# Layer 0's state products with large and small halves side by side in 256 columns, q divided before it is turned, sums held in PSUM, and a new order for layer 0

## The chip, the core and the metric

The program runs on one core of one Trainium2 chip. The metric is the device time of one execution, in microseconds (us). A core has a matmul engine (TensorE, PE in the profile, with its weight loads listed as PEld), and three engines for elementwise work: VectorE (DVE), ScalarE (ACT) and GpSimd (POOL). SyncE (SP) issues the DMAs here. Each engine takes its own instructions strictly in order and waits on semaphores for the others. Matmuls write to PSUM, which has eight banks of 512 float32 columns per partition; GpSimd does not use PSUM.

## The reference

Two attention layers follow each other, for 8 batches of 512 tokens and width 512. Layer 0 is the linear kind: q gets a softmax within each head, k a softmax over the tokens, and the state is k transposed times v for each of 8 heads of 64.

```python
xn = _ln(x, ln_w, ln_b)
q = xn @ Wq + bq
k = xn @ Wk + bk + (1.0 - src_mask) * -1000000.0
q = jax.nn.softmax(q.reshape(b, t, h, dh), axis=-1)
k = jax.nn.softmax(k.reshape(b, t, h, dh), axis=1)
v = ((xn @ Wv + bv) * src_mask).reshape(b, t, h, dh)
att = jnp.einsum('bnhd,bnhl->bhdl', k, v)
y = jnp.einsum('bnhd,bhdl->bnhl', q, att).reshape(b, t, d)
emb_out = (jax.nn.silu(emb) @ W_emb + b_emb)[:, None, :]
scale, shift = jnp.split(emb_out, 2, axis=2)
hh = _ln(y, ln2_w, ln2_b) * (1.0 + scale) + shift
hh = jax.nn.silu(hh) @ W_out + b_out
return x + hh
```

Layer 1 has the same frame round an ordinary softmax attention with 16 heads of 32.

## The kernel before

Every float32 product is made from two rounded parts (`float32r`): a large part (name ending in h) and the small rest (l). A product A times B is three matmuls, Ah Bh, Ah Bl and Al Bh (`product`, L491). Each pass of `product` multiplies 128x128 weights with 512 columns.

The work of one batch in layer 0 is cut into named steps, and one list sets the order for all engines: `the_order` weaves tracks of steps by the guessed cost in `COST` and by start and end fractions. Each engine walks that list and issues its share. In a batch b of layer 0:

- `tx` turns x (16 transposes on PE), ACT writes the large part `xTh` and a full copy `tb` (L766, L769), DVE writes the rest `xTl` (L1024).
- `k` (16 passes, then on DVE mask and maximum, on ACT Exp into `ET`), `v` (16 passes; DVE adds the bias into `vt`, ACT writes `vh`, DVE writes `vl`: L1077, L802, L1080), `te` (turns `ET`; ACT writes `Eh`, DVE `El`, L785 and L1056), `q` (16 passes; DVE bias and maximum L1090 and L1094, POOL subtracts it L1284, ACT Exp into `eq` L809).
- `st` makes the state: for each of 4 column groups and 4 token tiles the three matmuls L581, L582, L583 with 128 columns. `sta` then scales it by the sums of k and splits it into `Ah` and `Al` (L1105, L817, L1110). `Ah` is 130 columns wide: two extra columns of ones make the sums of each q row on PE.
- In batch b+1's k stretch, `y` turns `eq`, splits it (`qh` on ACT L825, `ql` on DVE L1116), multiplies it with the state (L603, L604, L605, 130 columns), and DVE divides by the q sums (L1126, L1130).
- `ny` normalises y (statistics on DVE, L1277 on POOL), `ty` turns it and makes silu, with DVE writing into `yb` twice (L1140, L1143), ACT `sTh` (L842), DVE `sTl` (L1148). `o` (16 passes) multiplies with W_out; DVE adds x and SP stores.

PSUM banks are handed out in the same list (`the_banks`): eight banks rotate in the order in which they come free, and `done` names the semaphore that frees one. Layer 1 has its own table of fractions and is bounded by a chain of matmuls, maxima (L1170), exponentials (L885) and sums (L1325); it shares `tx`, `v`, `ty` and `o` with layer 0.

The state part of PE's program is

```python
for t in range(NT):
    e.matmul(bank[:, n], Eh[:, t, n], vh[:, t, n], start=(t == 0), stop=False)
    e.matmul(bank[:, n], Eh[:, t, n], vl[:, t, n], start=False, stop=False)
    r = e.matmul(bank[:, n], El[:, t, n], vh[:, t, n], start=False, stop=(t == NT - 1))
```

Of the kernel before, what the change touches and what calls it, by code (L numbers as in the profile page):

```python
# [5 lines left out]
ALU = mybir.AluOpType  # L6
ACT = mybir.ActivationFunctionType
# [22 lines left out]
    "k": MM + (0.0,), "v": MM + (0.1, 0.2, 0.0), "q": MM + (0.3, 0.0), "o": MM + (0.0,),  # L30
# [5 lines left out]
    "stacks": (0.0,), "ahead": (0.0,), "narrow": (0.0,), "end": (0.0,),  # L36
# [4 lines left out]
PLAN = {  # L41
    "att": ((0.03, 0.83), (0.03, 0.83), (0.1, 0.97), (0.03, 0.83)),
# [35 lines left out]
def the_order():  # L78
# [19 lines left out]
    for b in range(B):  # L98
        past, first, last = b >= 1, b == 0, b + 1 == B
        yb = [("y", b - 1, g) for g in range(5)] if past else []  # L100
        if last:
            o.append((("ahead",), 0))
        weave(o, (tiles("k", b), 0, 1), (yb, 0.05, 1), ([] if first else [("nx", b + 1)], 0.3, 0.9),
              (wpart(0, "v") if first else [], 0.2, 0.9), (first_m[0] if first else [], 0.9, 1.0))
        weave(o, (tiles("v", b), 0, 1), (tiles("te", b), 0.18, 0.85), ([("ny", b - 1)] if past else [], 0, 0.8),
# [66 lines left out]

def bank_uses(p, i):
# [50 lines left out]
def temp_uses(order):  # L224

    last, before = {}, {}
    for p, i in order:
        if i == 0 and (p[0] == "tx" or (p[0] == "ty" and p[2] < NC)):
            before[p] = last.get(p[2] % 2)
            last[p[2] % 2] = p  # L230
    return before


# [15 lines left out]
def cond_two_layers(nc, A, out):  # L249
# [4 lines left out]
    temp_before = temp_uses(order)  # L254
    with ctx:
# [61 lines left out]
        vh = sb("vh", [128, NT, D], FR, c=c0)  # L317
        vl = sb("vl", [128, NT, D], FR, c=c0)
# [5 lines left out]
        Ah = sb("Ah", [128, NC, 130], FR, c=c0)  # L324
        Al = sb("Al", [128, NC, 130], FR, c=c0)
# [8 lines left out]
        yrc = sb("yrc", [128, 2, 4], c=c0)  # L334
# [3 lines left out]
        for i in range(2):  # L338
# [17 lines left out]
            "att", "a_set", "A_sc", "A_hi", "A_lo", "q_tr", "qT_hi", "qT_lo", "y_mm", "y_rc", "y_sc",  # L356
# [17 lines left out]
        def temp_free(p):  # L374

            k = temp_before[p]
            if k is None:
                return None
            return s["xT_lo" if k[0] == "tx" else "y_s"], 4 * k[1] + k[2] + 1

        def done(key):
# [4 lines left out]
            if k == "v":  # L386
                return s["v_add"], 4 * key[1] + key[2] + 1
# [92 lines left out]
        def _(e):  # L480
# [1084 lines left out]
```

## Time and profile before

| | us |
|---|---|
| median of 3 runs | 1534.92 |
| their range | 1533.7 to 1539.51 |
| the profiled execution | 1538.86 |
| its span | 1536.9 |

| engine | busy us | share of the span |
|---|---|---|
| PE | 1430.6 | 93% |
| PEld | 1011.7 | 66% |
| DVE | 1018.9 | 66% |
| ACT | 776.9 | 51% |
| POOL | 757.4 | 49% |

The span is the time from the first to the last instruction; the profiled execution took 2 us more than its span. Matmuls overlap in the records: each lasts longer than the distance to the next one, so for PE the distance between starts is what to read, not the duration. A row of the timeline gives start, duration, engine, line and operation, and in brackets the idle time before it with what ended it. A row of the windows view gives a stretch and, for each engine, busy time and number of instructions in it, then the granted clock of PE as a share of full speed. Layer 0 runs from about 15 to 515 us, 61 us per batch, and layer 1 from there to the end.

### The profile page before, as it was taken

How to read it: one execution, taken by the hardware profiler on the slowest of the kernel's cores; microseconds unless marked ns; L12 is line 12 of the kernel's file. 1: busy time of each engine (PE TensorE's matmuls, PEld its weight loads, DVE VectorE, ACT ScalarE, POOL GpSimd, SP SyncE). 2: the span in 40 equal slices, each digit the busy share in tenths (PEclk: the TensorE clock that was granted, in tenths of full speed). 3: DMA queues.
4: the chain of work that ended last, by engine and by line, in shares of the span. 5: the costliest groups of instructions: out<-in, count | busy, mean ns of one | idle time of the engine just before them, and what ended most of it. 6: DMA issues, size and time to landing. Idle time of an engine off the chain costs nothing.

```text
span 1536.9 us, 21020 instructions
## 1 busy us (share of the span) xinstructions
PE 1430.6 (93%) x7296; PEld 1011.7 (66%) x7296; DVE 1018.9 (66%) x1929; ACT 776.9 (51%) x1305; POOL 757.4 (49%) x660
## 2 busy tenths in 40 slices
PE   6999999999999798998998998998998999999985
PEld 4788888888888675565565565565565665565543
DVE  5687777778778675647657557556656656746654
ACT  5334334334344435555646646645755655564561
POOL 0222333233222325557656765774675765846852
PEclk9899999999999899998999999999999999999996
DMA  8011121111222266553354335335434434533320
GB/s 311 5 58 55 35 90 55 35 55 35 90 76 69 70 172 178 164 138 103 96 125 130 103 106 149 92 104 144 109 90 140 122 97 124 131 103 97 106 73 28
DMA packets 83914, 156.19 MB, mean 102 GB/s; under 512 B 8264, under 2 KB 8264, under 8 KB 83808
## 3 DMA queue, kind: packets, MB, share of 16 engines
q1 hardware_dynamic: 83808, 154.84, 35.2%
q8 instruction: 58, 0.95, 0.3%
q14 instruction: 48, 0.39, 0.1%
HBM read 104.45 MB, written 50.36 MB: 101 GB/s over the span
## 4 chain that ended last, share of the span: by engine, by line
PE 66%; DVE 18%; issue 6%; POOL 5%; ACT 5%; DMA 0%; POOLq 0%; ACTq 0%; SPq 0%; DVEq 0%
PE ps L494 13%; PE ps L496 12%; PE ps L495 11%; PE ps L651 6%; PE ps L685 6%; PE ps L668 6%; DVE cT L1170 6%; PE ps L489 4%; DVE st L1011 3%; POOL yb L1277 2%; DVE yb L1143 1%; PE ps L706 1%; DVE yb L1140 1%; ACT Pb L885 1%; PE ps L605 1%
## 5 line engine op out<-in xcount | busy, mean ns | idle before, releaser
L1325 POOL TENSOR_TENSOR Pb<-Pb 128x512 f32<-128x512 f32 x376 | 471.0, 1293 | 182.9 <-PE ps L685 109.3
L1170 DVE TENSOR_REDUCE cT<-ps 128x1 f32<-128x512 f32 x512 | 325.5, 683 | 93.5 <-PE ps L651 93.3
L885 ACT ACTIVATE Pb<-ps 128x512 f32<-128x512 f32 x512 | 282.3, 611 | 204.6 <-PE ps L668 186.8
L651 PE MATMUL ps<-Ks,Qs 98*128 98x512 f32 x512 | 198.8, 433 | 16.3 <-DVE sg_q L1162 12.0
L668 PE MATMUL ps<-Qs,Ks 106*128 106x512 f32 x512 | 186.9, 417 | 5.6 <-ACT Qs L868 1.6
L651 PEld LDWEIGHTS ps<-Ks,Qs 98*128 98x128 f32 x512 | 97.0, 195 | 107.9 <-DVE cT L1170 40.9
L1256 POOL TENSOR_TENSOR rs<-ve,mhalf 128x4 f32<-128x4 f32 x32 | 33.0, 1032 | 248.3 <-DVE ve L997 152.8
L668 PEld LDWEIGHTS ps<-Qs,Ks 106*128 106x128 f32 x512 | 96.6, 190 | 63.6 <-ACT Pb L885 21.7
L1284 POOL TENSOR_TENSOR vt<-vt,qmx 128x512 f32<-128x512 f32 x32 | 33.4, 1045 | 163.1 <-DVE qmx L1094 163.1
L494 PE MATMUL ps<-Wh_o,sTh 128*128 128x512 f32 x256 | 109.8, 429 | 4.1 <-DVE sTl L1148 3.6
L494 PE MATMUL ps<-xTh,Wh_k 128*128 128x512 f32 x256 | 109.9, 429 | 1.6 <-DVE Wl_k L950 1.4
L494 PE MATMUL ps<-Wh_v,xTh 128*128 128x512 f32 x256 | 105.7, 413 | 0.0
L496 PE MATMUL ps<-Wh_o,sTl 128*128 128x512 f32 x256 | 104.3, 407 | 0.0
L495 PE MATMUL ps<-Wl_o,sTh 128*128 128x512 f32 x256 | 103.7, 405 | 0.0
L496 PE MATMUL ps<-xTh,Wl_k 128*128 128x512 f32 x256 | 103.1, 403 | 0.0
L495 PE MATMUL ps<-xTl,Wh_k 128*128 128x512 f32 x256 | 102.8, 401 | 0.0
L496 PE MATMUL ps<-Wh_v,xTl 128*128 128x512 f32 x256 | 100.8, 394 | 0.0
L495 PE MATMUL ps<-Wl_v,xTh 128*128 128x512 f32 x256 | 100.2, 391 | 0.0
L1291 POOL TENSOR_TENSOR wr<-wr,boB 128x512 f32<-128x512 f32 x64 | 93.4, 1478 | 12.7 <-DMA wr<-in_x 12.6
L1024 DVE TENSOR_TENSOR xTl<-tb,xTh 128x512 fp32r<-128x512 f32 x64 | 54.4, 850 | 60.9 <-ACT tb L769 60.9
L1156 DVE TENSOR_TENSOR wr<-ps,wr 128x512 f32<-128x512 f32 x64 | 43.9, 686 | 71.5 <-PE ps L496 71.3
L1162 DVE SCALAR_TENSOR_TENSOR sg_q<-ps,cols,sg_q 128x512 fp32r<-128x512 f32 x32 | 23.7, 742 | 89.3 <-ACT sg_q L860 89.3
(176 smaller groups left out, 3102.2 us busy)
## 6 DMA issues: line engine op xcount, KB each, us to landing
Qs<-stack_scratch SPq DMA_DIRECT2D x96, 256.0 KB
Ks<-stack_scratch SPq DMA_DIRECT2D x96, 256.0 KB
stack_scratch<-sg_q SPq DMA_DIRECT2D x32, 512.0 KB, 2.8
stack_scratch<-sg_k SPq DMA_DIRECT2D x32, 512.0 KB, 3.1
wr<-in_x SPq DMA_DIRECT2D x32, 256.0 KB, 5.3
x_scratch<-wr SPq DMA_DIRECT2D x32, 256.0 KB, 2.0
wr<-x_scratch SPq DMA_DIRECT2D x32, 256.0 KB, 3.7
out<-wr SPq DMA_DIRECT2D x32, 256.0 KB, 2.0
```

What stands on the lines that cost most here:

```text
L489: r = e.transpose(bank[:, t * 128:(t + 1) * 128], src, ident)
L494: e.matmul(bank[:], lh(k), rh(k), start=(k == 0), stop=False)
L495: e.matmul(bank[:], lh(k), rl(k), start=False, stop=False)
L496: return e.matmul(bank[:], ll(k), rh(k), start=False, stop=(k == NC - 1))
L651: e.matmul(bank[:], Qs[par][0:RX, j, t * 128:(t + 1) * 128], Ks[par][0:RX, j, :], start=True, stop=True).then_inc(s["S"], 1)
L668: e.matmul(bank[:], Ks[par][0:RE, j, m * 128:(m + 1) * 128], Qs[par][0:RE, j, :], start=True, stop=True).then_inc(s["ST"], 1)
L685: r = e.matmul(PV[32 * j:32 * j + 32, :], xbuf(8 + b)[:, m, h * 32:(h + 1) * 32], pb[:, j, :], start=(m == 0), stop=(m == NT - 1))
L885: e.activation(p_buf(n, m)[:, j, :], ps[bank_of["a", n, m, j]][:], ACT.Exp).then_inc(s["P"], 1)
L1024: e.tensor_tensor(xTl[:, c, :], tb[c % 2][:], xTh[:, c, :].bitcast(F32), ALU.subtract).then_inc(s["xT_lo"], 1)
L1170: e.tensor_reduce(nx[:, n % 2, j, t, 0:1], ps[bank_of["S", n, j, t]][:], AX.X, ALU.max, negate=True).then_inc(s["S_max"], 1)
L1291: e.tensor_tensor(wr[t][:], wr[t][:], boB[:], ALU.add).then_inc(s["xb"], 1)
L1325: e.tensor_tensor(acc[:, j, :], acc[:, j, :], p_buf(n, m)[:, j, :], ALU.add).then_inc(s["Ps_pool"], 1)
```

## The change

1. State and y products. `vh`/`vl` become one tile `vhl`, `Ah`/`Al` one tile `Ahl`, with the large and small part of the same 128 columns next to each other. The two matmuls with the same weights become one with 256 columns; its two halves land in separate columns of PSUM and are added afterwards. Two matmuls (256 and 128 columns) replace three. The state takes two banks instead of one.
2. The additions: ACT copies the small half out (`A_c1`, `y_c1`), DVE adds it to the large half (`A_sc`, `y_sc`).
3. The columns of ones are gone. q is divided by its sum before it is turned: a new step `qn` per token tile sums (DVE) and inverts (DVE), and POOL multiplies `eq`. The division by the k sums moves from the state into the copy of the turned q (`qh`, `ql`).
4. Intermediates stay in PSUM: the full copy of x (`xT_f`), v with its bias, and u in `ty` are written back into the bank they were read from, which stays taken for longer. `tb` and `vt` are no longer used there. This holds for layer 1 too.
5. The fractions for layer 0's tracks move into `PLAN` with new values, and GpSimd's memset of ones (`ones`) moves from `stacks` to behind the last `y`.

```diff
 PLAN = {
+    "0k": ((0.134, 0.71), (0.313, 1.065)),
+    "0v": ((0.56, 1.051), (0, 0.565)),
+    "0q": ((0.109, 0.992), (0, 0.247), (0.978, 0.998)),
...
-            return s[("k_exp", "v_lo", "q_exp")[r // 4]], 4 * c + r % 4 + 1
+            return s[("k_exp", "q_exp")[r // 4]], 4 * c + r % 4 + 1
...
             if k == "v":
-                return s["v_add"], 4 * key[1] + key[2] + 1
+                return s["v_lo" if key[1] < 8 else "v_hi"], 4 * key[1] + key[2] + 1
...
             if k == "ty":
-                return s["y_u"], 4 * key[1] + key[2] + 1
+                return s["s_lo" if in_bank(key[1]) else "y_s"], 4 * key[1] + key[2] + 1
...
                 for t in range(NT):
-                    e.matmul(bank[:, n], Eh[:, t, n], vh[:, t, n], start=(t == 0), stop=False)
-                    e.matmul(bank[:, n], Eh[:, t, n], vl[:, t, n], start=False, stop=False)
-                    r = e.matmul(bank[:, n], El[:, t, n], vh[:, t, n], start=False, stop=(t == NT - 1))
+                    e.matmul(out, Eh[:, t, n], vhl[:, t, :, n], start=(t == 0), stop=False)
+                    r = e.matmul(out[:, 0:128], El[:, t, n], vhl[:, t, 0, n], start=False, stop=(t == NT - 1))
...
-                        n, o_ = slice(t * 128, (t + 1) * 128), bank[:, u * 130:(u + 1) * 130]
-                        e.matmul(o_, a[:, n], Ah[:, g, :], start=True, stop=False)
-                        e.matmul(o_, a[:, n], Al[:, g, :], start=False, stop=False)
-                        r = e.matmul(o_, l[:, n], Ah[:, g, :], start=False, stop=True)
+                        n, o_ = slice(t * 128, (t + 1) * 128), bank[:, u * 256:(u + 1) * 256]
+                        e.matmul(o_, a[:, n], Ahl[:, g, :, :].rearrange("p s n -> p (s n)"), start=True, stop=False)
+                        r = e.matmul(o_[:, 0:128], l[:, n], Ahl[:, g, 0, :], start=False, stop=True)
...
-                    e.activation(tb[c % 2][:], bank[:], ACT.Identity, scale=p[:, c:c + 1], bias=p[:, 4 + c:5 + c]).then_inc(s["xT_f"], 1)
+                    e.wait_ge(s["xT_hi"], 4 * x + c + 1)
+                    e.activation(bank[:], bank[:], ACT.Identity, scale=p[:, c:c + 1], bias=p[:, 4 + c:5 + c]).then_inc(s["xT_f"], 1)
...
                         part = ps[bank_of["st", b, u]][r, :].rearrange("p (g s n) -> p g s n", g=2, s=2)
+                        e.copy(Af[r, 2 * u:2 * u + 2, :], part[:, :, 1, 64 * h:64 * h + 64]).then_inc(s["A_c1"], 1)
...
-                    e.copy(qh[g % 2][:], ps[bank_of["tq", b, g]][:]).then_inc(s["qT_hi"], 1)
+                    e.activation(qh[g % 2][:], ps[bank_of["tq", b, g]][:], ACT.Identity,
+                                 scale=krc[:, b % 2, g:g + 1]).then_inc(s["qT_hi"], 1)
...
+                    e.copy(yb[:, 2 * half:2 * half + 2, g * 128:(g + 1) * 128], y3[:, :, 1, :]).then_inc(s["y_c1"], 1)
...
-                    e.tensor_tensor(vt[t % 2 if x < 8 else 0][:], ps[bank_of["v", x, t]][:], bvB[:], ALU.add).then_inc(s["v_add"], 1)
+                    e.tensor_tensor(ps[bank_of["v", x, t]][:], ps[bank_of["v", x, t]][:], bvB[:], ALU.add).then_inc(s["v_add"], 1)
...
+            def qn(i, b, t):
+                n = 4 * b + t + 1
+                e.wait_ge(s["q_exp"], n)
+                e.tensor_reduce(qdn[:, t % 2, :], eq[:, t, :].rearrange("p (h d) -> p h d", h=H0), AX.X, ALU.add).then_inc(s["q_den"], 1)
...
+                e.reciprocal(qrc[:, t % 2, :], qdn[:, t % 2, :]).then_inc(s["q_rc"], 1)
...
+                    yv = yb[:, 2 * half:2 * half + 2, g * 128:(g + 1) * 128]
+                    e.tensor_tensor(yv, y3[:, :, 0, :], yv, ALU.add).then_inc(s["y_sc"], 1)
...
-                        e.tensor_scalar(yv, t4(ps[bank_of["ty", x, c]]), mod[:, 0, c, bb:bb + 1], mod[:, 1, c, bb:bb + 1],
+                        u = ps[bank_of["ty", x, c]]
+                        e.tensor_scalar(u[:], u[:], mod[:, 0, c, bb:bb + 1], mod[:, 1, c, bb:bb + 1],
```

How the new order stands on PE, at the border from v to q in batch 2 of layer 0 (psN are banks, `Wh_q,xTh` and its like are the passes of q, `identr,yb` turns y of the batch before, `vh,Eh` is the first state matmul). Before:

```order
L489 MATMUL ps3<-identr,yb 128x128 x4
L494 MATMUL ps6<-Wh_q,xTh 128x512
L495 MATMUL ps6<-Wl_q,xTh 128x512
L496 MATMUL ps6<-Wh_q,xTl 128x512
L494 MATMUL ps0<-Wh_q,xTh 128x512
L495 MATMUL ps0<-Wl_q,xTh 128x512
L496 MATMUL ps0<-Wh_q,xTl 128x512
L489 MATMUL ps7<-identr,yb 128x128 x4
L494 MATMUL ps0<-Wh_q,xTh 128x512
L495 MATMUL ps0<-Wl_q,xTh 128x512
L496 MATMUL ps0<-Wh_q,xTl 128x512
L581 MATMUL ps5<-vh,Eh 128x128
```

And now, from the last turn of the k exponentials (`identr,ET`):

```order
L486 MATMUL ps5<-identr,ET 128x128 x4
L491 MATMUL ps4<-Wh_q,xTh 128x512
L492 MATMUL ps4<-Wl_q,xTh 128x512
L493 MATMUL ps4<-Wh_q,xTl 128x512
L486 MATMUL ps0<-identr,yb 128x128 x4
L486 MATMUL ps3<-identr,yb 128x128 x4
L491 MATMUL ps4<-Wh_q,xTh 128x512
L492 MATMUL ps4<-Wl_q,xTh 128x512
L493 MATMUL ps4<-Wh_q,xTl 128x512
```

Behind the last row stand one more turn of y and then the first state matmul. Before, six passes of q and three turns of y stood between the last v product and the first state matmul; now the last turn of `ET`, two passes and three turns of y.

On PE at the start of batch 2's k stretch, where y of the batch before begins. Before, the second turn of `eq` with what follows it; the first turn stands three passes of k ahead of it:

```order
L489 MATMUL ps2<-identr,eq 128x128 x4
L494 MATMUL ps7<-xTh,Wh_k 128x512
L495 MATMUL ps7<-xTl,Wh_k 128x512
L496 MATMUL ps7<-xTh,Wl_k 128x512
L494 MATMUL ps7<-xTh,Wh_k 128x512
L495 MATMUL ps7<-xTl,Wh_k 128x512
L496 MATMUL ps7<-xTh,Wl_k 128x512
L603 MATMUL ps0<-Ah,qh0 128x130
```

Now, from the first turn:

```order
L486 MATMUL ps5<-identr,eq 128x128 x4
L491 MATMUL ps4<-xTh,Wh_k 128x512
L492 MATMUL ps4<-xTl,Wh_k 128x512
L493 MATMUL ps4<-xTh,Wl_k 128x512
L486 MATMUL ps1<-identr,eq 128x128 x4
L491 MATMUL ps0<-xTh,Wh_k 128x512
L492 MATMUL ps0<-xTl,Wh_k 128x512
L493 MATMUL ps0<-xTh,Wl_k 128x512
L600 MATMUL ps2<-Ahl,qh0 128x256
L601 MATMUL ps2<-Ahl,ql0 128x128
```

Between the first turn and the first y matmul there are two passes and one turn now, and five passes and one turn before.

On DVE at the border from q to o in batch 1. Before:

```order
L1090 TENSOR_TENSOR vt<-ps,bqB 128x512
L1094 TENSOR_REDUCE qmx<-vt 128x8
L1105 TENSOR_TENSOR Af<-ps,krc 64x256 x2
L1110 TENSOR_TENSOR Al<-Af,Ah 64x4x64 x2
L1024 TENSOR_TENSOR xTl<-tb,xTh 128x512
L1156 TENSOR_TENSOR wr<-ps,wr 128x512
```

And now, with the sums of q (`qdn`) and their inverses around the state's additions and splits:

```order
L1097 TENSOR_TENSOR vt<-ps,bqB 128x512
L1101 TENSOR_REDUCE qmx<-vt 128x8
L1107 TENSOR_REDUCE qdn<-eq 128x8
L1111 RECIPROCAL qrc<-qdn 128x8
L1107 TENSOR_REDUCE qdn<-eq 128x8
L1111 RECIPROCAL qrc<-qdn 128x8
L1119 TENSOR_TENSOR ps<-ps,Af 64x2x64 x4
L1126 TENSOR_TENSOR Ahl<-ps,Ahl 64x2x64 x4
L1107 TENSOR_REDUCE qdn<-eq 128x8
L1111 RECIPROCAL qrc<-qdn 128x8
L1036 TENSOR_TENSOR xTl<-ps,xTh 128x512
```

The four instructions of two `qn` steps stand ahead of the state's, so the state and the next batch's x come later in DVE's queue by their length.

## Rows read from the trace of the kernel before

**Rows 1.** Windows: stretch, busy us (count) of PE, PEld, DVE, ACT, POOL, clock

```profile
50.00:111.00 61.00, 57.28 (x299) 50.15 (x298) 43.63 (x114) 22.13 (x39) 17.99 (x22) 0.86 0.12 40
111.00:172.00 61.00, 60.88 (x346) 51.71 (x345) 48.51 (x102) 23.03 (x41) 20.17 (x20) 1.00 0.19 57
```

**Rows 2.** Waits of PE, 50 to 480 us: us in total, times, longest

```profile
PE ps L489 <- POOL xin L1268: 3.6, 1, 3.6
```

**Rows 3.** Timeline of PE, 281 to 284 us: start, duration

```profile
280.82 0.22 PE L603 MATMUL ps<-Ah,qh 128*128 128x130 f32 x1
280.88 0.27 PE L604 MATMUL ps<-Al,qh 128*128 128x130 f32 x1
280.99 0.27 PE L605 MATMUL ps<-Ah,ql 128*128 128x130 f32 x1
...
282.18 0.22 PE L603 MATMUL ps<-Ah,qh 128*128 128x130 f32 x1
...
283.31 0.39 PE L496 MATMUL ps<-Wh_v,xTl 128*128 128x512 f32 x1
283.54 0.39 PE L494 MATMUL ps<-Wh_v,xTh 128*128 128x512 f32 x1
```

**Rows 4.** Timeline of PE, 40 to 42 us: matmuls of 8 columns

```profile
40.55 1.03 PE L517 MATMUL ps<-pick,sp 128*128 128x8 f32 x8
41.43 0.48 PE L494 MATMUL ps<-Wh_v,xTh 128*128 128x512 f32 x1
```

**Rows 5.** Windows of batch 0's state and the stretches behind it

```profile
60.00:66.00 6.00, 2.66 (x13) 2.69 (x14) 1.77 (x3) 2.02 (x4) 5.20 (x6) 0.65 0.00 0
66.00:70.00 4.00, 4.00 (x21) 4.00 (x21) 1.42 (x3) 3.41 (x6) 0.00 (x0) 0.50 0.00 0
```

**Rows 6.** Timeline of PE, 64 to 65 us

```profile
64.33 0.41 PE L582 MATMUL ps<-vl,Eh 128*128 128x128 f32 x1
64.55 0.41 PE L583 MATMUL ps<-vh,El 128*128 128x128 f32 x1
```

**Rows 7.** Timeline of PE, end of v and first state matmul

```profile
295.46 0.39 PE L496 MATMUL ps<-Wh_v,xTl 128*128 128x512 f32 x1
...
301.50 0.22 PE L581 MATMUL ps<-vh,Eh 128*128 128x128 f32 x1
```

**Rows 8.** Timeline of ACT and DVE, the last v tile of that batch

```profile
296.70 0.72 ACT L802 ACTIVATE vh<-vt,mk 128x512 fp32r<-128x512 f32 x1 [1.77 <-DVE vt L1077]
```

**Rows 9.** The same on DVE

```profile
297.46 0.75 DVE L1080 SCALAR_TENSOR_TENSOR vl<-vt,mk,vh 128x512 fp32r<-128x512 f32 x1 [0.79 <-ACT vh L802]
```

**Rows 10.** Groups of DVE, 111 to 480 us: count, busy us, mean ns, idle before

```profile
L1024 DVE TENSOR_TENSOR xTl<-tb,xTh 128x512 fp32r<-128x512 f32 x24 | 25.4, 1058 | 9.8 <-ACT tb L769 9.8
L1094 DVE TENSOR_REDUCE qmx<-vt 128x8 f32<-128x512 f32 x24 | 16.5, 686 | 2.5
L1056 DVE TENSOR_TENSOR El<-ps,Eh 128x512 fp32r<-128x512 f32 x22 | 14.8, 675 | 0.0
L1126 DVE RECIPROCAL yrc<-ps 128x4 f32<-128x4 f32 x48 | 8.4, 174 | 10.5 <-PE ps L605 10.1 <-issue 0.2
L1031 DVE TENSOR_SCALAR mB<-mB 128x512 f32<-128x512 f32 x5 | 3.6, 730 | 0.0
```

**Rows 11.** Groups of POOL, 111 to 480 us

```profile
L1284 POOL TENSOR_TENSOR vt<-vt,qmx 128x512 f32<-128x512 f32 x24 | 25.1, 1045 | 98.8 <-DVE qmx L1094 98.8
```

**Rows 12.** Waits of PE from 600 to 1500 us, layer 1

```profile
PE ps L659 <- DVE nxs L1188: 21.0, 9, 2.7
```

**Rows 13.** Timeline of DVE in layer 1, 711 to 718 us

```profile
711.11 0.69 DVE L1143 SCALAR_TENSOR_TENSOR yb<-tb,yb 128x512 f32<-128x512 f32 x1
...
715.01 1.10 DVE L1143 SCALAR_TENSOR_TENSOR yb<-tb,yb 128x512 f32<-128x512 f32 x1
...
717.25 0.19 DVE L1188 TENSOR_REDUCE nxs<-cT 128x16 fp32r<-128x32 f32 x1
```

**Rows 14.** Groups of DVE, 590 to 1500 us

```profile
L1024 DVE TENSOR_TENSOR xTl<-tb,xTh 128x512 fp32r<-128x512 f32 x28 | 19.4, 692 | 34.3 <-ACT tb L769 34.3
```

More of the change, by code:

```diff
@@ L35 @@
     "tl": (0.2, 0.1, 0.9, 1.1), "tlx": (1.0, 0.0, 0.4, 0.4, 0.4, 0.4),
-    "stacks": (0.0,), "ahead": (0.0,), "narrow": (0.0,), "end": (0.0,),
+    "stacks": (0.0,), "ones": (0.0,), "ahead": (0.0,), "narrow": (0.0,), "end": (0.0,),
 }
 PLAN = {
+    "0k": ((0.134, 0.71), (0.313, 1.065)),
+    "0v": ((0.56, 1.051), (0, 0.565)),
+    "0q": ((0.109, 0.992), (0, 0.247), (0.978, 0.998)),
+    "0o": ((0.012, 0.839), (0.012, 0.907), (0.012, 0.288)),
     "att": ((0.03, 0.83), (0.03, 0.83), (0.1, 0.97), (0.03, 0.83)),
@@ L108, in the_order @@
         state = tiles("st", b) + [("sta", b)]
-        weave(o, (tiles("q", b), 0, 1), ([] if first else state, 0.35, 1),
-              ([("ty", b - 1, c) for c in range(5)] if past else [], 0, 0.75),
+        weave(o, (tiles("q", b), 0, 1), ([] if first else state, *PLAN["0q"][0]), ([("qn", b, 0), ("qn", b, 1)], *PLAN["0q"][2]),
+              ([("ty", b - 1, c) for c in range(5)] if past else [], *PLAN["0q"][1]),
               ([("mb", 0, 1)] if first else [], 0, 0.5), ([("nx", 1)] if first else [], 0.1, 0.7),
@@ L113, in the_order @@
         if not last:
-            weave(o, (tiles("o", b - 1) if past else state, 0.05, 1), (tiles("tx", b + 1), 0, 0.9),
-                  (wpart(0, "o") if first else [], 0.3, 1))
+            weave(o, (tiles("o", b - 1) if past else state, *PLAN["0o"][0]), (tiles("tx", b + 1), *PLAN["0o"][1]),
+                  (wpart(0, "o") if first else [], 0.3, 1), ([("qn", b, 2), ("qn", b, 3)], *PLAN["0o"][2]))
     o.append((("stacks",), 0))
     weave(o, (tiles("o", B - 2), 0, 0.5), (tiles("tx", 8), 0, 0.35), (wpart(1, "q"), 0, 0.5),
+          ([("qn", B - 1, 2), ("qn", B - 1, 3)], 0.02, 0.35),
           ([("y", B - 1, g) for g in range(5)], 0.45, 1), ([("qk", 0, 0), ("qk", 0, 1)], 0.65, 0.95))
+    o.append((("ones",), 0))
     o.append((("stack", 0), 0))
@@ L221, in the_banks @@
     return bank, before
[L224 to L231, printed above, removed]
 def raw_items():
@@ L831, in ty @@
                         e.wait_ge(s["e_mod"], 16 * (x // 8 + 1))
-                    if (f := temp_free(("ty", x, c))) is not None:
-                        e.wait_ge(*f)
+                    if n >= 2:
+                        e.wait_ge(s["y_s"], n - 1)
                     e.wait_ge(s["yn_tr"], n + 1)
@@ L1038, in k @@
                         if b >= 2:
-                            e.wait_ge(s["A_sc"], 2 * (b - 1))
-                    if (f := kvq_before(b, g)) is not None:
+                            e.wait_ge(s["A_sc"], 4 * (b - 1))
+                    if (f := kq_before(b, g)) is not None:
                         e.wait_ge(*f)
```

170 lines of the change are left out of this document (87 added, 83 removed).

## The prediction, made before the changed kernel was run

> **What bounds the kernel now.** I read the busy times by stretch first. In a steady batch of layer 0, 61 us, PE is busy for 60.88 us and DVE for 48.51 [rows 1]; then the waits of PE: over seven batches the only one of size is a single 3.6 us for x of batch 1 [rows 2]. So layer 0 is bounded by how fast PE issues, and the distances between starts are the prices. In [rows 3] a whole 512-column matmul takes 283.54 - 283.31 = 0.23 us. Between the L603 at 280.82 and that at 282.18 lie six small matmuls (130 columns) and one pass of k, three wide ones: 1.36 - 0.69 = 0.67 us, 0.111 each. The reader is to see that this is not the price of 130 columns: eight matmuls of 8 columns take 41.43 - 40.55 = 0.88 us, 0.11 each as well [rows 4]. So up to some width a matmul with new 128x128 weights costs 0.11 us whatever its columns.
>
> Two places leave the pattern. Batch 0's state runs at half clock: PE idles 3.6 us [rows 2], the granted clock averages 0.65 over 60 to 66 us and is 0.50 (1.2 of 2.4 GHz) over 66 to 70 although PE is busy throughout [rows 5], and small matmuls then start 64.55 - 64.33 = 0.21 us apart (0.213 over a run of them) [rows 6]. And layer 1 is bounded by a chain over several engines, not by PE.
>
> **The pairs in place of triples.** State: 16 triples in each of 8 batches; y: 16 in each of 8. A triple costs 3 x 0.111 = 0.333 us. A pair costs 0.111 for the 128-column matmul and W for the 256-column one, which no row shows. Below, W is 0.11 (the weights' price); above, the straight line through 128 columns at 0.111 and 512 at 0.231 gives 0.151. I take 0.116, half the price of 512 columns, since the floor in [rows 4] shows that the line's constant part is not added. A pair is 0.227, and each saves 0.106.
> - 7 batches of state and 7 of y at full clock: 224 x 0.106 = 23.7 us.
> - Batch 0's state: 16 triples at half clock are 10.2 us. The new order puts the first state group ahead of the turn that waits for x, so 4 pairs run inside the old idle time, and 12 pairs of 2 x 0.213 cost 5.1. Gain 5.1.
> - Batch 7's y lies where layer 1 begins, with other waits. I count its 16 pairs at the full-clock price, 1.7.
>
> The Trainium skill ("TensorE: Matmul & The Clock Gate", "Back-to-back issue gap") gives N/2.4 + 2.5 ns for an isolated matmul: 56 ns for 128 columns, 109 for 256. By that a triple would be 167 and a pair 165 ns, and the change would gain nothing on PE. Here 128 columns take 111 ns, so the isolated gap does not bound; its section on LDWEIGHTS (128 columns of weights / 1.2 = 107 ns) does agree with the 0.11 in both groups. A pair at 107 + 109 would save 0.117 and the first line would be an estimated 26.2 in place of 23.7.
>
> **New waits of PE.** With PE at 61 - 32 x 0.106 = 57.6 us per batch, what was hidden has less cover, and the order itself tightens two places.
> - v to state. Before, the first state matmul starts 301.50 - 295.69 = 5.8 us after the last v product has been issued, at 295.46 + 0.23 [rows 7], and `vl` of the last tile ends at 298.21 [rows 9]. Now only the last turn of `ET` (4 x 0.11), two passes (1.38) and three turns (1.32) lie between: 3.1 us. The chain it must cover: that turn done at 0.72 (0.44 and the tail of its last matmul), ACT's `Eh` at the 0.72 of [rows 8]: 1.44 us; DVE's `El` 0.68, the mask 0.73 [rows 10] and `vl` 0.75 [rows 9] behind it: 3.6 us. The wait is 0.5.
> - The first y matmul. Before, five passes and a turn cover the split of the turned q; now two passes and a turn, 1.82 us. The split is an ACT instruction with a scale, 0.72, and a DVE one with a scalar, 0.75, behind a tail of 0.3: 1.77. With what DVE has in its queue I take 0.3.
> Together 0.8 us in each of 7 batches: 5.6 us. The bounds are 0 (DVE a little earlier everywhere) and 2 us a batch.
>
> **DVE, ACT, POOL.** DVE gets four sums and inverses, 4 x (0.686 + 0.17), 3.4 us a batch; it loses 8 inverses of 0.174 = 1.4, and 4 x (1.058 - 0.686) = 1.5 as `xTl` no longer reads two SBUF tiles while POOL works [rows 10]. In layer 1 the same instruction took 0.692 [rows 14]. The state's additions and splits are twice as many at half the size, about even. So 48.5 becomes 49 of 57.6 us: 85%. ACT gets eight copies of 256 columns and the state's, some 5 us on its 23 [rows 1]; POOL four multiplications of 1.045 [rows 11] on its 20. None bounds. `qn` 0 and 1 delay DVE's state work and the next x by 1.7 us at the end of q; o's 16 passes and four turns (12.8 us on PE) come behind, with 7.2 us of DVE work (four `xTl`, four additions, the other two `qn`), and cover that. The state takes two banks, and v and ty stay in theirs until the split is done; counted in PE's program at these prices, 4.8 us or more lie between the step that gives up a bank and its next use. The moved `ones` I price at nothing, as POOL is busy for a third of a batch [rows 1]. If o's cover is gone, k's first pass would be late by up to those 1.7 us.
>
> **Layer 1.** Banks are held longer by one ACT or DVE instruction and I found none whose next user comes that soon. One gain: `L1143` reads two SBUF tiles and took 0.69 to 1.10 us and more under POOL's load; the one at 715.01 stands ahead of the last maximum, and so of `nxs` at 717.25 [rows 13], for which PE waits (21.0 us in 9 waits [rows 12]). With u in PSUM it should be 0.69: 0.41 x 7 = 2.9 us. Bounds 0 and 7.
>
> **The sum.** -23.7 - 5.1 - 1.7 + 5.6 - 2.9 = -27.8. The profiled execution took 1538.86 (span 1536.9), 3.9 above the median, so this is 1511.1 there and 1534.92 - 27.8 = 1507.1 for the median. Forecast **1507**.
>
> **Rivals.**
> 1. Columns are what is paid: 256 cost 0.222. For it, 128 columns and 2 x 0.111; against, the 8-column rows. Then all three gains on PE go: 1534.9 + 5.6 - 2.9 = 1537.6, no change. 5%.
> 2. DVE's waits come to the front. It is idle 61 - 48.5 = 12.5 us a batch, in part waiting for ACT (0.79 before `vl` [rows 9]) in a fixed order. If all of that stayed, a batch would be 49 + 12.5 = 61.5 us and nothing would be left; halfway, 2 us a batch: 1534.9 - 33.4 + 14 = 1515.5. 20%.
> 3. Slower: a new wait in each batch lets the clock fall. One wait of 3.6 us cost batch 0 more than itself: the stretch with it issued 299 matmuls against 346 [rows 1], 47/346 x 61 = 8.3 us. Seven of these: 1534.9 - 33.4 + 58.1 = 1559.6. Its place would be k's first pass behind `qn` and the state's work on DVE. It decides from a loss of 4.8 us a batch (33.4 / 7). Against it: the cover of o above. 5%.
> 4. The clock stays up in batch 0, as 0.9 us of the 3.6 are now filled. The state would run at 0.227 a pair: 2.4 us less, and the turns and passes behind it about as much: 1502. 10%.
>
> **How the numbers follow.** The forecast case has 60%. What a measurement of this kernel can tell from no change is about 0.5%, 7.7 us. W at its upper end adds 224 x 0.035 = 7.8, waits of 2 us add 8.4; no waits, W at 0.11 and 7 us in layer 1 take off 5.6, 1.3 and 4.1. The range 1497 to 1522 holds cases 2 and 4 and either end alone. Faster: 60 + 20 + 10 and a little of the rest, 0.91; the same 0.05; slower 0.04.
>
> **What would show it.** L579 and L600 start 0.116 us ahead of their partners at full clock, L580 and L601 0.111; a steady batch is 58.4 us; PE's waits list the first state matmul behind `vl` with about 0.5 us and the first y matmul behind `ql`; `xTl` in layer 0 takes 0.69; PE's wait for `nxs` falls from 21 to about 18 us. I am wrong if a 256-column matmul costs 0.15 or more, if PE's waits in layer 0 exceed 2 us a batch, or if layer 1 moves by more than 7 us.

## The result, and the profile after

The changed kernel takes 1495.74 us, the median of 4 runs (1493.2 to 1501.43), where the kernel before took 1534.57 in runs beside it. The ratio is 0.9746, 95% interval 0.9708 to 0.9783: 38.8 us less, where 27.8 were forecast, and 1.3 us below the range. The profiled execution took 1493.49 us, its span is 1491.7.

Windows of one steady batch of layer 0 in the changed kernel (columns as in [rows 1]):

```profile
243.50:302.00 58.50, 58.50 (x322) 49.66 (x321) 48.43 (x106) 28.50 (x57) 21.80 (x25) 1.00 0.19 59
```

PE has no idle time left; DVE is at 83%, ACT has got 28.5 us. The same batch of the kernel before:

```profile
257.00:319.30 62.30, 62.14 (x354) 52.91 (x353) 49.14 (x102) 24.28 (x43) 20.16 (x21) 1.00 0.16 56
```

A batch was 62.3 us there, not the 61 that I used, which was only the width of the windows in [rows 1]. Pairs of the state on PE, start and duration:

```profile
281.13 0.36 PE L579 MATMUL ps<-vhl,Eh 128*128 128x256 f32 x1
281.33 0.22 PE L580 MATMUL ps<-vhl,El 128*128 128x128 f32 x1
281.39 0.33 PE L579 MATMUL ps<-vhl,Eh 128*128 128x256 f32 x1
281.56 0.22 PE L580 MATMUL ps<-vhl,El 128*128 128x128 f32 x1
281.62 0.34 PE L579 MATMUL ps<-vhl,Eh 128*128 128x256 f32 x1
```

A pair repeats after 281.62 - 281.39 = 0.23 us, where a triple took 0.333 [rows 3]. The waits of PE from 50 to 480 us (total, times, longest), answering to [rows 2]:

```profile
PE ps L486 <- POOL xin L1275: 2.7, 1, 2.7
PE ps L600 <- DVE ql L1132: 1.5, 1, 1.5
PE ps L579 <- issue: 1.4, 1, 1.4
PE ps L491 <- DVE xTl L1036: 0.6, 1, 0.6
```

None of them comes back in each batch. Batch 0's state and what follows, answering to [rows 5]:

```profile
60.00:66.00 6.00, 3.35 (x20) 3.21 (x19) 4.30 (x8) 1.66 (x3) 6.00 (x8) 0.75 0.00 0
66.00:70.00 4.00, 4.00 (x22) 4.00 (x21) 2.38 (x6) 3.93 (x7) 3.19 (x4) 0.53 0.00 0
70.00:78.00 8.00, 5.98 (x33) 4.34 (x32) 6.99 (x16) 7.01 (x17) 0.43 (x1) 1.00 0.45 132
```

The granted clock is back at 1.00 from 70 us. The stretch at 0.50 was 17 us long before (61.7 to 78.8 us) and is 7 now (63.0 to 69.8).

DVE groups, `xTl` of layer 0 and u's product of layer 1, answering to [rows 10, 13]:

```profile
L1036 DVE TENSOR_TENSOR xTl<-ps,xTh 128x512 fp32r<-128x512 f32 x24 | 16.4, 684 | 3.1 <-ACT ps L764 3.1
...
L1151 DVE SCALAR_TENSOR_TENSOR yb<-tb,ps 128x512 f32<-128x512 f32 x28 | 19.2, 687 | 1.0
```

and the second one before, from 590 to 1500 us, which I had read at only two places:

```profile
L1143 DVE SCALAR_TENSOR_TENSOR yb<-tb,yb 128x512 f32<-128x512 f32 x28 | 36.9, 1316 | 1.0
```

By the times at which `xTl` of each batch starts, the profiled executions differ by 5.8 us at batch 2, then by 3.8 more per batch, 29.5 at batch 8, 31.3 at batch 9 and 45.2 at the end. So layer 0 gave 31 us. Layer 1 gave 14 between these two executions, 7 to 8 by the medians (38.8 - 31.3). Executions of one kernel differ, and they differ with the mean granted clock: the four of the changed kernel took 1493.2, 1493.5, 1498.0 and 1501.4 us at 0.973, 0.976, 0.970 and 0.965.

### The profile page after: what moved, and what is told of

It is laid out like the page before. It is cut to its first block, busy times and chain, and to the rows that moved or that the text cites. A ratio compares the mean times of both kernels' runs of the same rounds, so it can differ in the third digit from the quotient of the medians.

```text
span 1491.7 us, 20585 instructions
## 1 busy us (share of the span) xinstructions
PE 1387.8 (93%) x7040; PEld 969.7 (65%) x7040; DVE 999.6 (67%) x1958; ACT 811.8 (54%) x1417; POOL 772.1 (52%) x692
## 4 chain that ended last, share of the span: by engine, by line
PE 66%; DVE 16%; ACT 8%; issue 5%; POOL 3%; DMA 1%; SPq 0%; POOLq 0%; ACTq 0%; DVEq 0%
PE ps L491 13%; PE ps L493 12%; PE ps L492 12%; PE ps L647 7%; PE ps L681 7%; PE ps L664 6%; DVE cT L1177 6%; PE ps L486 4%; ACT xTh L762 2%; DVE st L1023 2%; ACT ps L764 2%; PE ps L702 1%; DVE ps L1148 1%; PE ps L600 1%; ACT Pb L901 1%
## 5 line engine op out<-in xcount | busy, mean ns | idle before, releaser
L1304 POOL TENSOR_TENSOR wr<-wr,boB 128x512 f32<-128x512 f32 x64 | 82.2, 1297 | 13.6 <-DMA wr<-in_x 13.6
L1169 DVE SCALAR_TENSOR_TENSOR sg_q<-ps,cols,sg_q 128x512 fp32r<-128x512 f32 x32 | 23.8, 742 | 88.5 <-ACT sg_q L876 88.5
L1036 DVE TENSOR_TENSOR xTl<-ps,xTh 128x512 fp32r<-128x512 f32 x64 | 44.0, 688 | 51.3 <-ACT ps L764 51.1
```

Of the source, the lines that this page charges most:

```text
L1036: e.tensor_tensor(xTl[:, c, :], ps[bank_of["tx", x, c]][:], xTh[:, c, :].bitcast(F32), ALU.subtract).then_inc(s["xT_lo"], 1)
L1304: e.tensor_tensor(wr[t][:], wr[t][:], boB[:], ALU.add).then_inc(s["xb"], 1)
```

## The experiments

Each run stands beside runs of the kernel before on its own chip. Times are compared as ratios to it, and a difference in us is that of ratios times 1534.6. The changed kernel stands at 0.9746, and the interval of its own ratio is 6 us either way, so a difference against it is known to 6 to 8 us; one between two of the other kernels to 3 to 5. The medians of the kernel before, by which the ratios are taken, lay between 1534.4 and 1538.1 us, both of these on the same chip. Where a difference is smaller than that, the delays in the traces decide.

**Pairs and order, a square of four kernels.** First, pairs undone:

```diff
-                    e.matmul(out, Eh[:, t, n], vhl[:, t, :, n], start=(t == 0), stop=False)
+                    e.matmul(out[:, 0:128], Eh[:, t, n], vhl[:, t, 0, n], start=(t == 0), stop=False)
+                    e.matmul(out[:, 128:256], Eh[:, t, n], vhl[:, t, 1, n], start=False, stop=False)
```

and the same in y.

> The changed kernel with one part undone: each 256-column matmul of the state and of y is two of 128 columns again (same weights, same halves, same PSUM columns); order, q's division and all else stay. If the pairs are the gain of layer 0 (0.333 us for a triple, 0.230 for a pair in the trace), 224 pairs at full clock cost 224 x 0.103 = 23 us, batch 0's 16 cost 3 to 5 and batch 7's y 1.7: the time rises by 28 to 30 us, to about 1524, and a steady batch of layer 0 goes from 58.5 to 61.8 us. If the new order is the gain and PE's small matmuls have slack around them, it rises by less than 15 us.

Measured: 1527.12 us, ratio 0.9920 (0.9897 to 0.9942), +26.7 us. Then the order undone:

```diff
-    "0k": ((0.134, 0.71), (0.313, 1.065)), "0v": ((0.56, 1.051), (0, 0.565)),
-    "0q": ((0.109, 0.992), (0, 0.247), ..., "0o": ((0.012, 0.839), (0.012, 0.907), ...
+    "0k": ((0.05, 1), (0.3, 0.9)), "0v": ((0.18, 0.85), (0, 0.8)),
+    "0q": ((0.35, 1), (0, 0.75), ..., "0o": ((0.05, 1), (0, 0.9), ...
```

> The changed kernel with layer 0's tracks at the fractions of the kernel before (the two new q steps stay where they are). The prediction charged the new order with 5.6 us of waits, which the trace does not show. If the order was put right for the new lengths, the old one costs: the waits of PE in layer 0 grow by 0.5 to 2 us a batch and the time rises by 4 to 14 us. If the order carries nothing, the time stays within 2 us of the changed kernel. If my charge was real and hidden only in other terms, the time falls by up to 5 us.

Measured: 1527.17 us, ratio 0.9923 (0.9895 to 0.9950), +27.2 us: twice what I thought possible. Then both:

> The changed kernel with both parts undone: 128-column triples and the old fractions; what is left of the change is the division of q, the sums in PSUM and the copies on ACT. It closes the square of order and pairs: undoing the pairs alone cost 26.7 us and undoing the order alone 27.2. If the two gains are independent, this costs 54 us, 15 slower than the kernel before. If each hides the other (with triples PE is late enough for the old order's waits to be covered, and with the old order the pairs' time is waited away), it costs little more than either alone, 27 to 39 us, and a steady batch of layer 0 is again 62 us with few waits.

Measured: 1531.46 us, ratio 0.9965 (0.9951 to 0.9979), +33.6 us. So in the old order the pairs are worth 33.6 - 27.2 = 6.4 us, and with triples the new order is worth 6.9; together they are worth 33.6. The delays at batch 8 in the traces say the same: 22.6, 24.1 and 30.3 us. Each is the condition of the other. With both undone, what is left of the change still makes the kernel 5.4 us faster than the one before. One batch of the first kernel (new order, triples) and of the second (old order, pairs) in windows shows why:

```profile
254.60:316.40 61.80, 61.80 (x353) 53.04 (x352) 48.42 (x107) 28.76 (x57) 21.80 (x25) 1.00 0.18 56
```

```profile
252.60:314.40 61.80, 59.28 (x322) 49.53 (x321) 48.24 (x107) 27.96 (x57) 22.09 (x25) 1.00 0.18 56
```

The same 61.8 us, once with PE busy throughout, once with the pairs' time returned as idle time. The waits of PE in the second, 111 to 480 us:

```profile
PE ps L600 <- DVE ql L1132: 7.9, 6, 1.9
PE ps L486 <- ACT ET L772: 7.6, 6, 1.4
```

ACT's last exponential is late because its input is. DVE there (idle time and what ended it in brackets):

```profile
214.20 1.09 DVE L1140 TENSOR_TENSOR yb<-ps,yb 128x256 f32<-128x256 f32 x3 [1.14 <-ACT yb L841]
215.21 0.68 DVE L1058 CUSTOM_DVE_ANT_0 vt<-ps,mB 128x512 f32<-128x512 f32 x1
```

DVE idles 1.14 us for ACT's copy of the small half of y, a hand-over that part 2 of the change brought, with k's last maximum (L1058) queued behind it. This is the mechanism of my second rival; with the new order, all else equal, neither wait is there. Which stretch does it? Two of the four were tried alone, v and k:

> The changed kernel with the old fractions in the v stretch alone (the turns of the exponentials begin at 0.18 of it again and not at 0.56). With all the old fractions PE waited 1.27 us a batch for the last exponential (ET) before those turns. If that wait comes from the turns' place, this alone brings it back: 7 x 1.3 = 9 us or somewhat more. If it comes from what stands ahead on ACT (y's copies in the k stretch), this alone brings less than 3 us.

> The changed kernel with the old fractions in the k stretch alone (y from 0.05 to 1 of it and not from 0.134 to 0.71). With all the old fractions PE waited 1.2 us a batch at the first y matmul for the split of the turned q. If the wait comes from y's early start, this alone brings 7 x 1.2 = 8 to 10 us. And y's eight copies then end late in ACT's queue, ahead of the last exponential: if that is what made ET late, PE waits for it here too, and the cost is 14 us or more.

Measured: 0.9809 (0.9781 to 0.9837) and 0.9766 (0.9726 to 0.9806), by the medians +9.7 and +3.1 us, but up to batch 8 their traces are only 2.9 and 6.1 us late, against 24.1 with all the old fractions. PE's wait for `ET` is 0.5 us over six batches with the old v alone and absent with the old k alone. So neither of these two makes it alone. For v the trace fits the second case that I had set (less than 3 us), for k neither; the stretches of q and o were not tried alone, and which combination is the least is open.

**Batch 0.** The state behind the turn again, in batch 0 alone:

```diff
-            weave(o, (tiles("o", b - 1) if past else state, *PLAN["0o"][0]), (tiles("tx", b + 1), *PLAN["0o"][1]),
+            weave(o, (tiles("o", b - 1), *PLAN["0o"][0]) if past else (state, 0.05, 1), (tiles("tx", b + 1), *(PLAN["0o"][1] if past else (0, 0.9))),
```

> The changed kernel with batch 0's state behind the turn that waits for x of batch 1, as in the kernel before; nothing else moves. The prediction put about 2 us of its 5.1 on the four pairs that run inside the old idle time. If the shorter wait (2.7 for 3.6 us) also keeps the clock up (7 us of half clock there against 17.5), this costs 5 us or more; if only the four pairs moved, 1 to 2 us; if neither, nothing.

Measured: 1499.64 us, ratio 0.9748 (0.9728 to 0.9769): nothing, and batch 2's `xTl` starts within 0.3 us of the changed kernel's. The four pairs in the idle time gain nothing. The length of the half clock there goes with the pairs: in the seven kernels with triples (the kernel before included) that stretch is 10 to 17 us long, in the ten with pairs and no dummies at that wait 3 to 7 in all. Why it does is not shown.

**Widths.** A series behind the last o (its weights differ from one matmul to the next):

```diff
+            for width in (8, 64, 128, 192, 256, 320, 384, 448, 512):
+                for i in range(24):
+                    probe(width, i)
```

> The changed kernel with a series behind its last o: 48 matmuls of 512 columns, then 24 each of 8, 64, 128, 192, 256, 320, 384, 448 and 512 columns, each with other 128x128 weights, then 12 pairs of 256 and 128 columns. The whole is longer by the series, so only the distances between starts are read. If a matmul costs the larger of the weights' price and its columns, 8 to 256 columns are 0.11 to 0.12 us apart, 512 are 0.23, and 384 lie at 0.17. If a fixed part is added to the columns, 256 lies near 0.15. A pair should be 0.227 to 0.231.

Measured, in a single run, mean distance between starts in us: 8 columns 0.108, 256 0.120, 320 0.147, 384 0.174, 448 0.206, 512 0.229; a pair 0.227. The 64, 128 and 192 came out at 0.18 to 0.215, for the reason that the windows show (busy time and count of PE, then the granted clock), in the middle of the 8, 64 and 128 columns, at the end of the 192, and in the middle of the 256 and 384:

```profile
1500.00:1505.00 5.00, 5.00 (x28) 1.00 0.00 0
...
1507.00:1511.00 4.00, 4.00 (x24) 0.58 0.00 0
1511.50:1516.00 4.50, 4.50 (x23) 0.50 0.00 0
...
1521.20:1521.30 0.10, 0.10 (x2) 0.65 0.00 0
1521.30:1521.40 0.10, 0.10 (x3) 1.00 0.00 0
1521.50:1524.00 2.50, 2.50 (x23) 1.00 0.03 7
...
1528.00:1531.50 3.50, 3.50 (x22) 1.00 0.00 0
```

(The first row is the 512-column lead-in and the start of the 8 columns.) PE is busy for every bit of these windows, and still the clock falls, at 1507.6 us, 0.8 us into the 64 columns. It stays at half through the 128 and the 192 columns and is full again from 1521.3, when the last of the 192 columns start (at 1521.31) and before the first of the 256 (1521.42). Why it fell and rose at these places is not shown. Above 256 columns the time goes by columns: 0.229 for 512, 0.174 for 384; below lies a floor of 0.11. The Trainium skill ("TensorE: Matmul & The Clock Gate", "Back-to-back issue gap") has N/2.4 + 2.5 ns, 109 for 256 columns, as the isolated gap; with new weights each time the series shows 120. The 107 ns that follow from its section on LDWEIGHTS (128 columns / 1.2) are close to the floor.

**Layer 1: u in PSUM.** Undone in the changed kernel for batches 8 to 14, and done alone in the kernel before:

```diff
-                        e.tensor_scalar(u[:], u[:], mod[:, 0, c, bb:bb + 1], ...
...
+                        u = src[:] if in_bank(x) else yb[:, :, c * 128:(c + 1) * 128]
+                        e.tensor_scalar(u, ..., mod[:, 0, c, bb:bb + 1], ...
```

(`src` is the bank.) The bank of `ty` is given up one instruction sooner with u in SBUF, and one later with u in PSUM.

> The changed kernel with one part undone in layer 1: for batches 8 to 14 u is written into yb again, so that the instruction after it reads two SBUF tiles and the bank is given up one instruction sooner. If this read is what moved layer 1 (1.32 us on average against 0.69), it goes back to 1.3 us, PE's wait for nxs in the fifth, ninth, ... chain step grows from 2.3 to 2.7 us, the granted clock falls behind it again as in the kernel before, and the time rises by 7 to 10 us. If my term was right in size it rises by 3 us. If layer 1 gained from something else (x or v held in PSUM), it stays within 1 us.

> The kernel before with that one part of the change alone: in layer 1 u stays in the PSUM bank. If it is the whole gain of layer 1, the time falls by 7 to 10 us, to about 1526, and the low-clock stretches of 7 us behind the wait for nxs shrink or go. If my term was right in size it falls by 3 us; if something else moved layer 1, by less than 1 us.

Measured: 1503.82 us, 0.9769 (0.9745 to 0.9793), +3.5 us against the changed kernel, and 1532.91 us, 0.9967 (0.9950 to 0.9984), 5.1 us less than the kernel before. The part gives `yb<-tb,yb` back its 1327 ns and takes it to 686 in the other, so the whole change of that instruction is this part's. The first time, known to 7 us, decides nothing, and the second lies between the two stories.

What the length of that instruction depends on can be read exactly. The third and fourth of a batch on DVE in the kernel before (the first, at 711.11, and the second, at 715.01, stand in [rows 13]), and what GpSimd does then:

```profile
718.18 1.70 DVE L1143 SCALAR_TENSOR_TENSOR yb<-tb,yb 128x512 f32<-128x512 f32 x1
...
720.64 1.79 DVE L1143 SCALAR_TENSOR_TENSOR yb<-tb,yb 128x512 f32<-128x512 f32 x1
```

```profile
714.28 1.27 POOL L1291 TENSOR_TENSOR wr<-wr,boB 128x512 f32<-128x512 f32 x1
...
718.05 1.28 POOL L1291 TENSOR_TENSOR wr<-wr,boB 128x512 f32<-128x512 f32 x1
720.61 1.27 POOL L1304 TENSOR_TENSOR sTl<-yb,sTh 128x512 fp32r<-128x512 f32 x1 [1.28 <-ACT sTh L842]
```

The first of the four runs while GpSimd is idle and takes 0.69. Each of the others starts while a GpSimd instruction runs and ends about 0.55 us after it: 715.55 and 716.11, 719.33 and 719.88, 721.88 and 722.43. It is so for all 23 that start beside a GpSimd instruction in batches 8 to 15 of this trace. In the changed kernel, with u in PSUM, they take 0.69 beside the same work. So the four of a batch take 0.69, 1.07, 1.71 and 1.79 us, 2.5 more than four of 0.69, and 2.1 of these lie on the third and fourth.

**The clock in layer 1.** From batch 1 of layer 1 on, PE waits for long twice in each batch: 1.7 us for `sg_q`, the small half of q, and 2.3 (before: 2.7) for `nxs`, the reduced maxima. In the changed kernel the half clock follows 9 of these 14 waits, at least one in each batch; in the kernel before 11 of 14. Dummy matmuls ahead of both waits (here the second; 14 stand ahead of the first), written into the bank that the waiting matmul overwrites:

```diff
+                    if n % 4 == 1 and n > 4:
+                        for _ in range(18):
+                            e.matmul(bank[:, 0:128], identr[:], identr[:], start=True, stop=True)
                     e.wait_ge(s["nx_lo"], n + 1)
```

> The kernel before with dummy matmuls ahead of the two waits of PE that come back in each batch of layer 1 from the second on (14 of 128 columns before the first S matmul, 18 before the one that reads nxs, written into the bank that the waiting matmul overwrites): at 0.11 us each they last 1.5 and 2.0 us, a little less than the waits of 1.7 and 2.7 us. If the idle time itself is what makes the clock fall, the half-clock stretches behind these waits shrink or go, and the time falls by up to 7 batches x (3.5 + 7) us / 2 = 30 us, by 10 us or more. If the clock follows something else, the time does not fall, and it rises by what the dummies overrun the wait, 0 to 5 us.

> The changed kernel with the same dummy matmuls. The waits are 1.7 and 2.3 us and the low-clock stretches behind them 3.5 us and, in some batches, 3.5 us more. If idle time makes the clock fall, the time falls by 5 to 15 us, to about 1485, and this version beats both kernels. If the clock follows something else, it stays or rises by up to 5 us.

Measured: in the kernel before 1528.76 us, ratio 0.9938 (0.9926 to 0.9950), 9.5 us less. In the changed kernel **1481.03**, ratio 0.9628 (0.9616 to 0.9640), 18 us below the changed kernel by the ratios, 14.7 by the medians and 12.2 between the two traces: the fastest kernel here. Its four runs lie within 0.9 us, those of the changed kernel within 8, and from x of batch 10 to x of batch 15 each batch takes 115.9 to 116.2 us, where it took 117.0 to 118.5. 26 us of batch 9, changed kernel and changed kernel with dummies (the dummies are among the counts, and the second kernel is 3 us further on in its batch):

```profile
666.00:692.00 26.00, 21.71 (x104) 13.93 (x103) 21.64 (x43) 17.25 (x28) 20.60 (x19) 0.93 0.52 142
```

```profile
666.00:692.00 26.00, 24.83 (x135) 15.67 (x133) 21.26 (x40) 18.22 (x30) 21.63 (x19) 1.00 0.56 152
```

With the idle time filled the clock stays up behind these waits: between 600 and 1440 us the changed kernel has 31 us at half clock, the one with dummies 1. What the dummies leave of the two waits (17.0 and 12.0 us) is 0.9 and 4.3. PE's waits from 600 to 1440 us, changed kernel and with dummies:

```profile
PE ps L655 <- DVE nxs L1195: 17.0, 8, 2.3
PE ps L647 <- DVE sg_q L1169: 12.0, 7, 1.7
```

```profile
PE ps L650 <- ACT Pb L907: 4.5, 14, 0.4
PE ps L650 <- DVE sg_q L1175: 4.3, 7, 0.6
...
PE ps L661 <- DVE nxs L1201: 0.9, 1, 0.9
```

Then dummies at the other long waits, 42 of 512 columns before the last y among them:

> The changed kernel with the dummies of the earlier run, and further ones of 512 columns (0.23 us each) ahead of PE's other long waits, each a little shorter than its wait: 10 before x of batch 1 (2.7 us), 26 before the first turn of batch 7's q (6.4), 6 before batch 7's y (1.7), 15 and 5 before the second and third nxs (3.7 and 1.4), and 42 before the last y (10.6). 45 us of half clock were left there. If idle time is what lowers the clock in these places too, the time falls by 5 to 15 us below the earlier 1481; if they are bounded by other engines' chains, it stays within 2 us of it.

Measured: 1481.67 us, ratio 0.9642 (0.9621 to 0.9664), no gain. The half clock of the whole execution went from 51 to 15 us, the mean clock of the last 39 us from 0.74 to 0.90, and nothing came of it. By what I had set before the run, those places are bounded by other engines' chains; which ones was not traced.

**The sizes with the clock held.** The three undoings and the mirror once more, each with the two groups of dummies, against 0.9628 (and 0.9938 for the kernel before):

> The changed kernel with the dummies ahead of the two waits (1481.0 us) and, in layer 1, u in yb again. Without half-clock stretches behind the waits the DVE instruction that reads two SBUF tiles costs its own length: 1.32 - 0.69 = 0.63 us ahead of nxs in 7 batches is 4.4 us, and up to four of them on the chain are 10 to 17 us at most. If the term of the prediction was mis-sized by the clock alone, this costs 3 to 5 us. If the instruction is on the chain more than once in a batch, 8 to 12 us.

> The kernel before with the dummies (1528.8 us) and u of layer 1 in PSUM. The mirror of the run above: 3 to 5 us faster than 1528.8 if only the clock blew the term up, 8 to 12 if the instruction is on the chain more than once a batch.

> The changed kernel with the dummies and with 128-column triples for the pairs. Layer 0 alone should carry it: 3.3 us in 7 batches and 5 in batch 0 and batch 7's y, 28 us: about 1509. If the pairs also touched layer 1 (by when its waits fall), it differs from that by more than 3 us.

> The changed kernel with the dummies and with the old fractions. In its trace layer 0 was 24 us longer and layer 1 began 24 us later; the rest of its 27 us was the clock. So 23 to 26 us here, about 1505.

| kernel with dummies | us | ratio (95%) | against its base | delay in the trace at batch 8, 10, 15, end, us |
|---|---|---|---|---|
| changed, u in SBUF | 1495.93 | 0.9742 (0.9719 to 0.9765) | +17.5 | -0.2, 4.0, 13.0, 15.9 |
| before, u in PSUM | 1514.91 | 0.9872 (0.9848 to 0.9895) | -10.1 | -2.6, -6.2, -14.8, -19.6 |
| changed, triples | 1508.21 | 0.9823 (0.9800 to 0.9846) | +29.9 | 23.8, 25.8, 25.9, 25.7 |
| changed, old order | 1503.75 | 0.9792 (0.9769 to 0.9814) | +25.2 | 21.0, 22.4, 22.6, 22.2 |

Pairs and order act in layer 0 alone; their delay is constant through layer 1. u in SBUF costs 9.0 us over five batches (10 to 15), 1.8 in each, and u in PSUM gains 8.6 over the same five. (The -2.6 at batch 8 of the second row is not this part's: batch 0's half clock was 13.7 us long there and 17.1 in its base.) The delay arises at one place in each batch. Read in batch 12 of the second row and its base: up to the second u instruction the maxima keep step to 0.1 us; then `nxs` is 0.4 us apart, and the first maximum behind the fourth 1.8. So of the 2.5 us that the four are longer 1.8 reach the chain, 0.4 by the second, which is the one that I had priced, and the rest by the third and fourth. In layer 1 the two traces have 16.1 and 17.0 us, the ratios 17.5 and 10.1 (each known to 4 us), the medians themselves 14.9 and 13.9. The term is 10 to 17 us, where I had 2.9 and expected 3 to 5 even here.

## Why the prediction was wrong, step by step

- **Pairs for triples**: right. 0.230 a pair against 0.227, so 224 x 0.103 = 23.1 us. The split was off: in the records L580 starts 0.17 behind L579 and the next L579 0.06 behind it, not 0.116 and 0.111; only the sum can be read. Rival 1 (columns are paid) is out, and the straight line to 0.151 too: 256 columns alone take 0.120.
- **Batch 0**: 5.1 forecast, about 2.0 measured: `xTl` of batch 1 starts 0.5 us later and that of batch 2 5.8 earlier; the 5.8 less a steady batch's 3.8 are 2.0. The clock did come back nine microseconds sooner, somewhat as rival 4 had it, but from 70 to 78 us PE is busy for 5.98 of 8 us now: what the clock gave was returned as idle time, with DVE and ACT at 7 of 8 us. And the four pairs moved into the old idle time gain nothing.
- **New waits of PE**, +5.6: the first failed step. There are none in a steady batch. I priced the new order as a cost and the pairs as a gain of their own. The runs show the reverse: in the old order PE waits 2.6 us a batch (`ET` and `ql`), and the pairs bring 6.4 us. The sum for the wait between v and state missed by a little: I set 3.6 us of chain against 3.1 of cover between the last turn of `ET` and the state. In the changed kernel that turn starts at 278.07 and the first state matmul at 281.13, 3.06 us; DVE between them:

```profile
279.32 0.69 DVE L1068 TENSOR_TENSOR El<-ps,Eh 128x512 fp32r<-128x512 f32 x1 [0.35 <-ACT Eh L780]
279.93 0.42 DVE L1043 TENSOR_SCALAR mB<-mB 128x512 f32<-128x512 f32 x1
280.26 0.74 DVE L1087 SCALAR_TENSOR_TENSOR vhl<-ps,mk,vhl 128x512 fp32r<-128x512 f32 x1
```

The chain ends at 281.00, after 2.93 us: 0.13 us to spare. Of the 0.67 that I had too much 0.31 are the mask (0.42 where its group had 0.73), 0.19 the turn and `Eh` (1.25 for 1.44), and the rest is that each DVE instruction starts a little before the one ahead of it has ended. In this order the wait is absent by a narrow margin. The 0.3 for the first y matmul is not there either: PE waits for `ql` once (1.5 us) from 50 to 480 us.
- **The base**: I began from 61 us a batch. The kernel before took 62.3, the kernel with triples in the new order 61.8: 0.5 in each of 7 batches, 3.5 us, that the change gained and no term of mine had. With triples in the old order a batch is 62.2, so most of it goes with the order; as idle time of PE it does not show (62.14 of 62.30 busy). That a steady batch came out at 58.5 where I had 58.4 is luck: a base 1.3 too low, and 0.8 of waits that did not come and 0.5 of delay that went, stand against each other.
- **Layer 1**, -2.9: the second failed step, mis-sized. I took 1.10 us from one row, the second instruction of a batch, and no other. For `nxs` this was right: PE's longest wait for it fell from 2.7 to 2.3. But the third and fourth were at 1.71 and 1.79 and reach the chain behind `nxs`. With dummies at the waits the part is worth 10 to 17 us. In the kernels as they are, 3.5 and 5.1 us were measured by the ratios; that half-clock stretches take back the rest is argued, not shown. The layer as such is not reproducible: in seven profiled kernels with the same instructions in it, it lasted 895 to 907 us from batch 9's x to the end, and 885 to 886 in the three with dummies at both waits. By my own sign ("if layer 1 moves by more than 7 us") this step was wrong.
- Together: 23.1 (pairs) + 3.5 (base) + 2.0 (batch 0) + 1.8 (batch 7's y, 1.7 forecast) is 30.4 of the 31.3 in layer 0, and 7 to 8 are left for layer 1. So of the 11 us between forecast and measurement 5.6 are the waits, 4.6 layer 1, 3.5 the base and 0.9 not attributed; batch 0 and the pairs take 3.7 off again.
- **The range** held each low end by itself. All three together (no waits, W at 0.11, 7 us in layer 1) are 11 us and give 1496.1, below its 1497, and that is about what came.
- Rival 3 (a wait in each batch lets the clock fall) did not come in layer 0, not even with the waits of the old order (clock 1.00 in the window above). `xTl` at 0.69 was right (0.684); PE's waits for `nxs` from 600 to 1440 us fell from 20.1 to 17.0, 3.1 where 2.9 were forecast ([rows 12] has 21.0 up to 1500).

How much of layer 1's gain a given execution keeps depends on where the half-clock stretches fall; what sets their place is open.

## What to carry to other kernels

Where PE is bound and DVE is at 80%, an edit that shortens PE's work and the order that lets it show are one change: run the square of both before giving either a price, and charge the hand-overs (here ACT's copy, then DVE's addition) to what is queued behind them. Take the length of every instruction of a group in a batch, not of one, and look at what GpSimd does beside each: here one was 0.69 us and the next ones up to 1.79. When a term lies behind waits at which the clock falls, fill the waits with dummies first and measure then: the four runs of the changed kernel lay within 8 us and those with dummies within 0.9, and the dummies themselves were worth 12 to 18 us.

## What the runs showed of the hardware

- With new 128x128 weights, at the full clock, a matmul costs 0.108 us for 8 columns and 0.120 for 256; from there it goes by columns (0.147 for 320, 0.174 for 384, 0.229 for 512). A pair of 256 and 128 columns takes 0.227 to 0.230.
- With PE busy without a gap the granted clock fell from 1.00 to 0.50 at 1507.6 us, in the 64-column series behind the 8-column one, and was 1.00 again from 1521.3, at the end of the 192-column series. Batch 0's state was at half clock for 10 to 17 us in the kernels with triples and for 3 to 7 in those with pairs.
- Idle time of 1.7 us at PE was followed by 3.4 us of half clock in six of seven batches of the changed kernel, idle time of 2.3 us in three of seven; with 14 and 18 dummies of 128 columns in its place there was none.
- A DVE instruction with two SBUF inputs that started while a GpSimd instruction on SBUF ran ended 0.55 us after that one, in 23 of 23 cases, and took 0.69 us with GpSimd idle; with one input in PSUM it took 0.69 beside GpSimd's work too. The means were 1316 and 687 ns. This agrees with the Trainium skill ("GPSIMD Engine Reference", the table of "Specifications"), by which GpSimd's SBUF interfaces are shared with VectorE and contended for by instructions with two SBUF inputs.
